# A four-layer transformer kernel: its instruction queues laid down a second time, and a QR's reflections moved to a line of their own

## The reference

```python
# layers 0, 1 and 2, each with sh, sc, g rows from silu(cond) @ w_ada + b_ada
h = layernorm(x) * (1 + sc_msa) + sh_msa
qkv = h @ w_qkv + b_qkv                      # 16 heads of 18
# layers 0 and 2: every head attends over the 256 tokens of its image
# layer 1: every token attends over its own 16 heads
x = x + g_msa * (attention(q, k, v) @ w_proj + b_proj)
h = layernorm(x) * (1 + sc_mlp) + sh_mlp
# layer 0: 4 experts of 288 -> 1152 -> 288, the two best of each token; layers 1 and 2: one such MLP
x = x + g_mlp * mlp(h)

# layer 3
U, _ = jnp.linalg.qr(P)                      # P is 288 x 64
A = skew(silu(cond) @ W.T + b)               # 64 x 64 for each image
R = expm(A)
z = x @ U
return x + (z @ R - z) @ U.T
```

## Time and profile before

| | |
|---|---|
| median of 3 runs | 1548.58 us (1545.59 to 1550.38) |
| the profiled execution, its own time | 1545.17 us |
| its span, first to last instruction | 1543.1 us |
| mean granted TensorE clock | 0.952 of 2.4 GHz |
| TensorE busy | 1367.0 us (89%) |
| DVE busy | 950.9 us (62%) |
| ACT busy | 818.6 us (53%) |
| POOL busy | 397.8 us (26%) |
| SyncE | issues DMAs only; the 16 DMA engines moved 91.82 MB |

### The profile page before, as it was taken

How to read it: one execution, slowest core, us unless ns; L and a number is a source line. 1 busy time by engine, 2 the same in 40 slices (tenths; PEclk the granted TensorE clock), 3 DMA queues, 4 the chain that set the end, 5 groups by cost and what they waited for, 6 DMA issues and landing times.

```text
span 1543.1 us, 30439 instructions
## 1 busy us (share of the span) xinstructions
PE 1367.0 (89%) x11841; PEld 822.0 (53%) x11841; DVE 950.9 (62%) x2315; ACT 818.6 (53%) x1597; POOL 397.8 (26%) x571
## 2 busy tenths in 40 slices
PE   4667999897999989999899988788899989998988
PEld 2333555563655545655466554455465556555655
DVE  5666877746567555555465555766777866656453
ACT  2555655657566424653345433675555665654542
POOL 1122232213233221222231322232332423321110
PEclk9887999998999999999999999899999999998998
DMA  5122234452213120321113122230000120000010
GB/s 154 48 65 92 83 102 136 149 158 86 65 43 104 38 76 8 75 80 62 51 24 96 44 75 83 51 67 13 17 9 5 36 74 13 5 7 13 1 39 31
DMA packets 76740, 91.82 MB, mean 60 GB/s; under 512 B 38989, under 2 KB 69814, under 8 KB 73270
## 3 DMA queue, kind: packets, MB, share of 16 engines
q1 hardware_dynamic: 74486, 87.52, 19.6%
q10 hardware_dynamic: 2112, 2.36, 0.5%
HBM read 73.22 MB, written 16.38 MB: 58 GB/s over the span
## 4 chain that ended last, share of the span: by engine, by line
PE 60%; DVE 13%; issue 10%; ACT 5%; DMA 5%; POOL 4%; SPq 2%; DVEq 0%; POOLq 0%; ACTq 0%
PE P L1346 27%; PE P L1506 4%; PE P L1508 4%; PE P L1507 4%; PE P L1475 3%; DVE NM L1776 3%; PE P L1466 2%; PE P L1373 2%; PE P L1442 2%; PE P L1523 1%; POOL N L2225 1%; PE P L1363 1%; POOL X L2210 1%; PE P L1517 1%; DVE AT L1908 1%
## 5 line engine op out<-in xcount | busy, mean ns | idle before, releaser
L1346 PE MATMUL P<-XT,W 128*128 128x512 f16 x1512 | 355.5, 387 | 6.1 <-DVE NM L1776 2.6
L2210 POOL TENSOR_TENSOR X<-X,TM 128x288 f32<-128x288 f32 x144 | 122.0, 847 | 660.3 <-DVE TM L1851 438.8
L1506 PE MATMUL P<-W,H 128*128 128x288 f16 x864 | 252.9, 293 | 1.1 <-DVE H L1845 1.0
L1507 PE MATMUL P<-W,H 128*128 128x288 f16 x864 | 252.4, 292 | 0.0
L1508 PE MATMUL P<-W,H 128*128 128x288 f16 x864 | 252.3, 292 | 0.0
L1346 PEld LDWEIGHTS P<-XT,W 128*128 128x128 f16 x1512 | 143.8, 99 | 180.5 <-issue 21.3
L2118 ACT ACTIVATE ARENA<-P 128x512 f32<-128x512 f32 x256 | 136.7, 596 | 122.7 <-PE P L1466 122.2
L2128 ACT ACTIVATE G<-P 128x512 f32<-128x512 f32 x216 | 128.4, 594 | 126.9 <-PE P L1346 115.8
L1776 DVE TENSOR_REDUCE NM<-P 128x2 f16<-128x512 f32 x256 | 159.8, 686 | 3.5 <-PE P L1451 2.9
L1845 DVE TENSOR_TENSOR H<-G,H 128x512 f16<-128x512 f32 x138 | 98.9, 719 | 82.0 <-ACT H L2129 81.5
L1346 PE MATMUL P<-WQ,XT 128*128 128x288 f16 x1008 | 143.6, 294 | 1.5 <-DVE NM L1776 0.9
(11 more groups left out here) (307 smaller groups left out, 2232.1 us busy)
## 6 DMA issues: line engine op xcount, KB each, us to landing
W<-scr_w SPq DMA_DIRECT2D x9, 1440.0 KB, 6.0
W<-scr_w SPq DMA_DIRECT2D x9, 1368.0 KB, 5.9
scr_w<-W SPq DMA_DIRECT2D x4, 1440.0 KB, 6.4
scr_w<-W SPq DMA_DIRECT2D x4, 1368.0 KB, 5.7
STG<-in_L_w SPq DMA_DIRECT2D x8, 576.0 KB, 4.3
STG<-in_L_w SPq DMA_DIRECT2D x9, 432.0 KB, 4.1
STG<-in_L_WT SPq DMA_DIRECT2D x11, 324.0 KB, 4.2
G<-scr_ada SPq DMA_DIRECT2D x24, 144.0 KB, 3.7
```

The costliest lines, as they stand in the source:

```text
L1346: ins = e.matmul(o, l, r, start=k == 0, stop=k == len(pairs_) - 1)
L1506: e.matmul(o, hi, W2[:, 2 * m, :], start=False, stop=False)
L1507: e.matmul(o, hi, W2[:, 2 * m + 1, :], start=False, stop=False)
L2210: e.tensor_tensor(X[:, t, :], X[:, t, :], TM[st["k"]][:, :], ALU.add).then_inc(st.sem)
```

## The change

1. A function `by_readiness` runs over all five queues once `deal` has ended, and lays them down again. In each queue the steps are sorted into groups that keep their order: those of one semaphore, on ACT all those that need a function table as one group (`TABLES`), and all of SP's transfers as one group. Then it goes forward in time: of the first steps of the groups whose inputs have ended, each queue proposes the one that can begin first; where several can begin within 0.1 us (`NEAR`) of the queue's clock, the one that came first in the old order. The queue whose proposal begins first takes it. Banks and buffers stay as `deal` gave them, and the waits stay with the steps.
2. `householder` is taken out of the background line and is a line of its own with rank 4, the first in the list, which can begin at time zero. The exponentials follow the skew matrices in the background line at once.
3. In a reflection DVE has four instructions instead of ten: dot product, reciprocal, factor, update. POOL has five instead of one: sign, root, signed norm, the sum of the signed norm and column j of `BC` (in place, before the dot product), and the divisor. ACT squares straight from PSUM, with a factor of 2 before the square, so that the root is twice the norm, for the sign is now plus or minus a half. The signed norms are kept in a new 64 x 64 tile `NB`, and its diagonal is added to `AT` once at the end, in `hh_v`, which has four instructions instead of two. `hh_root` waits for the previous reflection's `hh_step`, and `hh_step` begins only after POOL's fourth instruction.
4. Prices are changed all over the plan, and `SLACK` and `BIAS` (the handicap of ACT where DVE could copy too).

```diff
-SLACK, BIAS = -0.68, 0.18
+NEAR = 0.1
+TABLES = dict(exps="exp", t_exp="exp", g_exp="exp", gelu="gelu", silu="silu")
+SLACK, BIAS = -0.6, 0.2
 
+def by_readiness(lanes):
+    queues, table = [], None
+    for lane in lanes:
+        some = {}
+        for k, st in enumerate(lane.steps):
+            st.index, st.end = k, None
+            name = "dma" if lane.name == "sp" else "table" if st.kind in TABLES else id(st.sem)
+            some.setdefault(name, deque()).append(st)
+        queues.append(list(some.values()))
+        lane.steps, lane.clock = [], 0.0
+    while True:
+        best = None
+        for lane, some in zip(lanes, queues):
+            mine = None
+            for qu in some:
+                if qu and all(x.end is not None for x in qu[0].deps):
+                    begin = max(lane.clock, max((x.end for x in qu[0].deps), default=0.0) + LAT)
+                    key = (begin if begin > lane.clock + NEAR else lane.clock, qu[0].index)
+                    if mine is None or key < mine[0]:
+                        mine = key, begin, qu
+            if mine and (best is None or mine[1] < best[0]):
+                best = mine[1], lane, mine[2]
+        if best is None:
+            return
+        begin, lane, qu = best
+        st = qu.popleft()
+        if st.kind in TABLES and TABLES[st.kind] != table:
+            table, begin = TABLES[st.kind], begin + TAB
+        lane.clock = begin + st.cost
+        st.end = lane.clock + st.tail
+        lane.steps.append(st)
...
-            return n * max(0.058, cols / 2240 * wide + 0.003)
+            return n * max(0.058, cols / 2230 * wide + 0.001)
...
-            hi = do(act, "x_hi", 1.0, b=b, js=(j, j2), src=m, free=before)
+            hi = do(act, "x_hi", 0.86, b=b, js=(j, j2), src=m, free=before)
...
-                m = do(pe, "t_av", 1.05, u=u, c=c, i=i, j=j, js=js, e=ready, free=[jf, jsf], v=tok["v", b])
+                m = do(pe, "t_av", 0.55, u=u, c=c, i=i, j=j, js=js, e=ready, free=[jf, jsf], v=tok["v", b])
...
-                    got.append(do(act, "exps", 0.6, j=j, s=s, h=(2 * c + par) % 4, src=m, free=ef))
+                    got.append(do(act, "exps", 0.5, j=j, s=s, h=(2 * c + par) % 4, src=m, free=ef))
...
-                a = do(act, "gelu", 1.26, L=L, m=m, j=j, gi=gi, src=mt, free=[gf, h_rd[0]])
+                a = do(act, "gelu", 1.02, L=L, m=m, j=j, gi=gi, src=mt, free=[gf, h_rd[0]])
...
-                m = do(pe, "hh_mm", mm_cost(1, C - j, 4) + 0.1, c=j, j=c, src=last, free=pf)
+                m = do(pe, "hh_mm", 0.1 + (C - j) * 0.0017, c=j, j=c, src=last, free=pf)
                 yield
-                a = do(act, "hh_row", 0.55, incs=2, c=j, j=c, src=m, free=last if j else None)
+                a = do(act, "hh_row", 0.95, incs=2, c=j, j=c, src=m, free=last if j else None)
...
-                p = do(pool, "hh_root", 0.67, src=a, half=hp)
-                d = do(dve, "hh_step", 2.7, incs=10, c=j, src=a, root=p, at=p_in)
+                p = do(pool, "hh_root", 2.0, incs=5, c=j, src=a, half=hp, free=last if j else None)
+                yield [p]
+                d = do(dve, "hh_step", 1.4, incs=4, c=j, src=a, root=p, at=p_in)
...
-        bg = Line(chain(n0, wp_load(0), wg_load(), w1_load(0, 0), w2_load(0, 0), retire(), vrows(), ada(1), ada(2), skew(), householder(), expm_steps()), 3)
+        bg = Line(chain(n0, wp_load(0), wg_load(), w1_load(0, 0), w2_load(0, 0), retire(), vrows(), ada(1), ada(2), skew(), expm_steps()), 3)
...
-        deal([loads, attends, ends_, tops, preps, bg, *(Line(rotated(k), 5) for k in range(2))])
+        deal([Line(householder(), 4), loads, attends, ends_, tops, preps, bg, *(Line(rotated(k), 5) for k in range(2))])
+
+        by_readiness([pe, dve, act, pool, sp])
...
             def hh_step(st):
                 j = st["c"]
-                bc, aj, a1 = BC[:, j:C], AT[:, j:C], AT[:, j:j + 1]
-                nb, sg, g, rt, w, d = (HS[:, k:k + 1] for k in range(6))
-                q.wait_ge(st["src"], st["at"], (st.sem, st.first) if st.first else None)
-                e.tensor_tensor_reduce(out=HQ[:, j:C], in0=bc, in1=aj, scale=1.0, scalar=0.0, op0=ALU.mult, op1=ALU.add, accum_out=d).then_inc(st.sem)
-                e.tensor_scalar(sg, bc[:, 0:1], 0.0, 2.0, ALU.is_ge, ALU.mult).then_inc(st.sem)
-                q.wait_ge(st["root"], st.at(2))
-                e.scalar_tensor_tensor(out=nb, in0=sg, scalar=1.0, in1=N2[:, 1:2], op0=ALU.subtract, op1=ALU.mult).then_inc(st.sem)
+                bc, aj = BC[:, j:C], AT[:, j:C]
+                g, rt, w = (HS[:, k:k + 1] for k in range(3))
+                q.wait_ge(st["src"], st["at"], st["root"].at(4), (st.sem, st.first) if st.first else None)
+                e.tensor_tensor_reduce(out=HQ[:, j:C], in0=bc, in1=aj, scale=1.0, scalar=0.0, op0=ALU.mult, op1=ALU.add, accum_out=w).then_inc(st.sem)
+                q.wait_ge(st["root"])
+                e.reciprocal(rt, TI[:, j:j + 1]).then_inc(st.sem)
+                q.wait_ge(consts, st.at(2))
+                e.scalar_tensor_tensor(out=g, in0=w, scalar=rt, in1=NMK[:, j:j + 1], op0=ALU.mult, op1=ALU.mult).then_inc(st.sem)
                 q.wait_ge(st.at(3))
-                e.scalar_tensor_tensor(out=TI[:, j:j + 1], in0=nb, scalar=bc[:, 0:1], in1=N2[:, 0:1], op0=ALU.mult, op1=ALU.add).then_inc(st.sem)
...
                 e.scalar_tensor_tensor(out=aj, in0=bc, scalar=g, in1=aj, op0=ALU.mult, op1=ALU.add).then_inc(st.sem)
...
-                q.wait_ge(st.at(1))
-                e.activation(SQ[:, c:C], BC[:, c:C], ACT.Square, accum_out=N2[:, 0:1]).then_inc(st.sem)
+                e.activation(SQ[:, c:C], bank(st)[0:D, 0:C - c], ACT.Square, scale=2.0, accum_out=N2[:, 0:1]).then_inc(st.sem)
...
             def hh_root(st):
-                q.wait_ge(st["src"], st["half"])
+                first, nb = BC[:, st["c"]:st["c"] + 1], NB[:, st["c"]:st["c"] + 1]
+                q.wait_ge(st["src"], st["half"], st["free"])
+                e.tensor_scalar(N2[:, 2:3], first, 0.0, 0.5, ALU.is_ge, ALU.subtract).then_inc(st.sem)
                 e.tensor_tensor(N2[:, 1:2], N2[:, 0:1], HP[:, :], ALU.pow).then_inc(st.sem)
+                q.wait_ge(st.at(2))
+                e.tensor_tensor(nb, N2[:, 2:3], N2[:, 1:2], ALU.mult).then_inc(st.sem)
+                q.wait_ge(st.at(3))
+                e.tensor_tensor(first, first, nb, ALU.add).then_inc(st.sem)
+                q.wait_ge(st.at(4))
+                e.tensor_tensor(TI[:, st["c"]:st["c"] + 1], nb, first, ALU.mult).then_inc(st.sem)
```

More of the change, by code:

```diff
@@ L1 @@
+from collections import deque
 from contextlib import ExitStack
@@ L159, in do @@
             newest[0] = max(newest[0], st.end)
+            st.cost, st.tail, st.deps = cost, st.end - lane.clock, [x for v in fields.values() if isinstance(v, (Step, list, tuple)) for x in flat(v) if isinstance(x, Step)]
             lane.steps.append(st)
@@ L362, in split_cols @@
                     else:
-                        x = do(act, "w_hi3", 0.2 + (b - a) * 0.00085, dst=dst, rows=96 if bias is None else 128, a=a, b=b, scale=s, i=i, src=ld, free=before)
+                        x = do(act, "w_hi3", 0.15 + (b - a) * 0.00085, dst=dst, rows=96 if bias is None else 128, a=a, b=b, scale=s, i=i, src=ld, free=before)
                         y = do(dve, "w_lo3", 0.1 + (b - a) * 0.0011, dst=dst, rows=32 if bias is None else 64, a=a, b=b, scale=s, i=i, src=ld, hi=x)
@@ L489, in layernorm @@
                 s = do(dve, "ln_stats", 0.45, w=w, n=n, t=t, x=XW[t], free=tok.get(("st", w)))
-                aggr.append(do(dve, "ln_aggr", 0.18, w=w, n=n, src=s, free=tok.get(("mv", w))))
+                aggr.append(do(dve, "ln_aggr", 0.13, w=w, n=n, src=s, free=tok.get(("mv", w))))
             tok["st", w] = list(aggr)
@@ L503, in layernorm @@
             _, j2, pf2 = rP.take()
-            m = do(pe, "xb_T", 0.8, y=YL[w], js=(j, j2), full=z, free=[pf, pf2])
+            m = do(pe, "xb_T", 0.82, y=YL[w], js=(j, j2), full=z, free=[pf, pf2])
             rYL[w].free[0] = [m]
@@ L536, in turned @@
                 yield [m]
-                v = copy("tq" if name == "q" else "tk", 1.03 + BIAS, 1.22, u=u, g=g, j=j, src=m, free=free)
+                v = copy("tq" if name == "q" else "tk", 0.97 + BIAS, 1.14, u=u, g=g, j=j, src=m, free=free)
                 rP.free[j] = [v]
@@ L623, in heads @@
                 yield [m]
-                a = do(act, name + "_hi", 0.66, n=n, j=j, src=m, free=last[n])
+                a = do(act, name + "_hi", 0.56, n=n, j=j, src=m, free=last[n])
                 yield [a]
-                d = do(dve, name + "_lo", 0.46, n=n, j=j, src=m, hi=a, free=last[n])
+                d = do(dve, name + "_lo", 0.42, n=n, j=j, src=m, hi=a, free=last[n])
                 rP.free[j] = [a, d]
@@ L638, in heads @@
                 yield [m]
-                v = copy("qt" if name == "q" else "kt", 1.03 + BIAS, 0.7, u=u, n=n, j=j, src=m, free=(qt_rd if name == "q" else kt_rd)[u])
```

(20 more changed lines are left out.)

56 lines of the change are left out of this document (25 added, 31 removed).

## The result

The changed kernel takes 1447.74 us (median of 4 runs, 1447.58 to 1451.14) beside 1549.48 us for the kernel before in the same job: a ratio of 0.9352, 95% interval 0.9328 to 0.9375. The forecast of 1491 us was 43 us too high.

A forecast was written before the change was run, and what follows sets the result against it. TensorE's work, its 176.1 us of idleness and its lower clock were taken to bound the kernel; -12 - 8 - 24 - 23 - 8 + 2 + 15 = -58 us from 1545.2 gave 1487, plus 3.4 for the median 1491 us, range 1466 to 1516.

The forecast's parts named there:

- the rival's 1446 us: Rival that nearly all of TensorE's gaps are filled, by gains beyond the forecast's: 1446 us, chance 0.14.
- the whole range: The prediction's outer range for the measured time, 1446 to 1545 us.
- The second laying: All five queues, 150 to 1473 us: a third of TensorE's other 69 us of idleness goes, 23 us gained, bounds 0 and 50.
- its missing margin: Second pass wants inputs no earlier than 0.08 us before use, so late ends hold queue heads: 15 us charged, bounds 0 and 50.
- the slower rival: TensorE's heads wait behind ACT's and DVE's evictions for lack of margin: about 1593 us, chance 0.10.
- Waits for a reflection: TensorE's 34.3 us of waits on the previous reflection's last DVE instruction: 24 us gained, bounds 0 and 34.
- Reflections from the beginning: Reflections on their own line fill TensorE's idleness in the first 150 us: 12 us gained, bounds 0 and 30.
- the sign by which I said that I'd be wrong: TensorE's idleness in the first 150 us staying at 56 us.
- Clock: TensorE spends 32 us less at the lower clock, half of them busy: 8 us gained, bounds 0 and 25.
- The exponential and the rotations: Exponential follows the skew matrices at some 385 us, first images' rotations fill gaps before 1473: 8 us gained, bounds 0 and 15.
- POOL: Four more POOL instructions per reflection, 51 us in all, can hold x_add and a layer norm: 2 us charged, bounds 0 and 12.
- DVE: Six instructions fewer per reflection, DVE from 950.9 to about 871 us busy, hidden by TensorE: no gain given.

The follow-up runs named there:

- b_pass2: The kernel before with the second laying of all five queues added, old prices and old reflections kept: 1478.7 us, ratio 0.955.
- a_pass_pe: The changed kernel whose second laying may swap steps on TensorE only: 1508.6 us, ratio 0.974.
- a_late: The changed kernel with the reflections' line held until the skew matrices are laid, and layer 2's first attention until layer 1's last output: 1460.7 us, ratio 0.944.
- a_nopass2: The changed kernel without its second laying: 1532.3 us, ratio 0.989.
- a_oldprices: The changed kernel with every price, `SLACK` and `BIAS` as before, except the reflections' prices: 1468.3 us, ratio 0.947.

## Why the prediction was right, and where it was not

The direction was right, and so was the main mechanism, TensorE's gaps filled by an order that passes over what is not ready: the second laying alone brings 70 us, and 85 on top of the rest. The sizes were not. The sum had 50 us less idleness and 8 us from the clock; measured are 67.3 and 29.8. So 17 us of the error are gaps and 22 are busy time, and 3.4 more were added for the median. TensorE's idleness, 108.8 us, is not far from the 115 to 130 that were forecast. That the whole lies at the rival's 1446 us is luck for the rival: of the 45 us that it took beyond the forecast only 8 or 9 were for the clock (half of 25 - 8), the rest for gaps. That it lies inside the whole range, by 1.7 us, is luck too.

- **The second laying** (I took -23, and +15 for its missing margin): too small. Alone it takes 47.4 us off the idleness (b_pass2), of which 31 are the reflections' waits (34.3 to 3.2). That leaves 16 us for 23 - 15 = 8; the rest of the 70 us is busy time, which I had put under the clock. In the kernel after, the idleness beyond the reflections' waits fell by 35.5 us, for which I had 26 in sum. I took a third of TensorE's other waits because I thought of it as a swap of matmuls in front of TensorE. a_pass_pe shows that this is the smaller part; 61 of 85 us need new orders of DVE, ACT and POOL too. A row for it was before me: DVE's waits for POOL and ACT inside and before a reflection, 31.8 us in front of L1899 and 24.6 in front of L1896, to which I gave nothing, since DVE is only 62% busy. In b_pass2 they are 12.0 and 30.0 us, 14 us less in sum, so these two waits are a small part of what the other queues' orders bring, and which part of those orders brings the rest is open. The charge for the margin has nothing behind it: TensorE's waits on DVE and ACT without the reflections' fell from 93 to 64 us, and the slower rival rested on their growing.
- **Waits for a reflection** (-24): 31.8 us are gone. I said that it takes prices which agree; b_pass2 gets 31 of them without.
- **Reflections from the beginning** (-12): the idleness of the first 150 us fell by 2.8 us, the sign by which I said that I'd be wrong. 9 reflections lie there, not 20 (x9 of L2262 before 150 us), and two mispriced steps at the head of TensorE's and DVE's queues cost what they bring. I had written that P's transfer is covered by the weights'; it lands at 16.8 us behind them and holds TensorE. a_late shows that without an early begin TensorE has been busy as long by 385 us.
- **Clock** (-8): the term that was off by most, -29.8 us of busy time for the same matmuls, some 25 of them by the clock. The time at 1.2 GHz falls by 53 us, from 148 us to (1 - 0.967) x 2 x 1446 = 95, where I took 32. I took half of that time as busy; 49.8 of the 53 us were. The earlier trace rows could have told: 14.40 of 15 us busy at a clock of 0.88. The gain lies where the gaps were already small: the clock stays low in the first 150 us (0.85, then 0.81), and behind them it goes from 0.96 and 0.97 to 0.99.
- **The exponential and the rotations** (-8): the squarings end at 500 us and the rotations begin 257 us earlier, as forecast. What that alone is worth was not tested. In a_late both the reflections and the rotations are late (first rotation at 1401 us), and it is 13 us slower than the kernel after: my 12 + 8 for the two terms together can be neither confirmed nor refused beside a scatter of 17. The last 91 us still idle 15.5.
- **POOL** (+2): the reflections hold POOL for 94 us instead of 43, the 51 us that I forecast, at 0.22 + 3 x 0.18 us for the new instructions. POOL is 419 us busy, not 450, because other work left it. DVE waits longer for x_add, 16.4 us in 24 where it was 3.9 in 12, and TensorE sees 0.8 us of it; but this isn't the roots' doing, as I had charged. It is 20.8 us in 26 in b_pass2, with one POOL instruction in a reflection, and 2.9 in 9 in a_nopass2, with five: it comes with the second laying. An update of `AT` of 1.38 us (L1945) began 0.07 us after a POOL subtraction of 1.16 us, and POOL's longest L2265, 1.14 us, began 0.19 us after a DVE subtraction of 0.67 us that another one followed, where their medians are 0.48 and 0.19. This fits the rule of the Trainium skill (SBUF — State Buffer, "SBUF: two separate sides") on the shared port, that the second one waits for the whole instruction, though the update ended 0.29 us after the subtraction and not its own 0.48. It changes nothing in the sum, as said.
- **DVE** (at no price): it is 902 us busy, not 871. Its six instructions are gone, and with them 83 us in the reflections, but its other work grew by some 31 us, which ACT and POOL had before: ACT fell from 818.6 to 788.8, POOL's work outside the reflections by 27 us. It doesn't take the new prices: with the old ones (a_oldprices) DVE is 902.8 us busy too. The short form was worth 72 us with the new prices and some 20, which can't be told from the scatter, with the old ones, and I gave it nothing. It is a term that I put at nothing because DVE's busy share is low, as with DVE's waits above.

## What to carry to other kernels

A pass that orders steps by when they can begin gained 24 us here on the busiest engine's queue alone and 85 on all five. So in queues that are executed in order, look also at the idle time in front of a waiting head on a half-idle engine, and ask which buffers its followers would free. The pass forgave a price that was 0.9 us too short, but not one that was wrong at the start, where nothing else is in flight. When gaps are filled, look at the busy time of the same matmuls too: almost a third of the gain came there, most of it from the clock. When a plan is made by a program, change a number without a meaning first, and read only the differences that are larger than what this does.

## What the runs showed of the hardware

- The same power instruction on POOL (64x1) takes less when another POOL instruction runs just before it: in the kernel before (L2225, median 703 ns in the earlier trace rows) 541 ns in the 31 cases where one ended less than 0.15 us earlier or ran on, 773 ns in the other 33; in the kernel after (L2263), where one always does, 553 ns.
- P's 64 rows land 10.4 us after their issue at 6.42 us, behind the first weights on the same queue (from 6 to 17 us the 16 DMA engines are busy throughout and move 318 GB/s), and 2.25 us after it at 383 us, where the DMA engines are busy for 0.25 of the time.
- A stretch can be busy and at the lower clock: of the 148.9 us at 1.2 GHz in the kernel before, TensorE was busy in 109.0.
